# An attention and top-2 expert block on one core: the expert stage in pairs of 128 slots with two experts, in place of tiles of 256 slots with one

## The reference

```python
logits = jnp.einsum('bsh,eh->bse', x, Wr)
top_v, top_i = jax.lax.top_k(jax.nn.softmax(logits, axis=-1), 2)
top_v = top_v / jnp.sum(top_v, axis=-1, keepdims=True)
for e in range(8):
    w_e = jnp.sum(jnp.where(top_i == e, top_v, 0.0), axis=-1)
    h = jax.nn.gelu(jnp.einsum('bsh,mh->bsm', x, W1[e]) + b1[e], approximate=False)
    y = jnp.einsum('bsm,hm->bsh', h, W2[e]) + b2[e]
    out = out + y * w_e[..., None]
```

## Time and profile before

| | |
|---|---|
| median of 3 runs | 680.27 us (679.78 to 681.35) |
| the profiled execution | 680.41 us |
| its span on the core | 678.7 us |
| PE busy | 615.8 us, 91% of the span |
| DVE busy | 465.7 us, 69% |
| ACT busy | 449.9 us, 66% |
| POOL busy | 418.0 us, 62% |
| expert stage on PE | from 256.4 to 507.5 us |

### The profile page before, as it was taken

One profiled execution on the slowest core, in us unless ns is written; L12 is line 12 of the kernel. 1 busy time (PEld: TensorE's weight loads), 2 busy tenths in 40 slices (PEclk: granted clock), 3 DMA queues, 4 the chain that ended last, 5 costly groups with the idle time before them and its releaser, 6 DMA issues. The chain is left out here.

```text
span 678.7 us, 21454 instructions
## 1 busy us (share of the span) xinstructions
PE 615.8 (91%) x7417; PEld 411.7 (61%) x7417; DVE 465.7 (69%) x1312; ACT 449.9 (66%) x689; POOL 418.0 (62%) x584
## 2 busy tenths in 40 slices
PE   2877558999999999999999999999999999999965
PEld 2755323444444438999999999999984444444423
DVE  7799986766676776445545446777566687878826
ACT  3999546888888884444444444444449888888854
POOL 6355627778777787775600027677737777677771
PEclk9899968999999999999999999999999999999989
DMA  5997685655445578855432335444536375556621
GB/s 160 297 288 228 185 248 111 109 108 104 115 115 118 125 126 199 206 143 143 108 88 71 73 88 120 112 115 118 120 78 104 84 137 116 121 124 139 122 68 32
DMA packets 186592, 89.36 MB, mean 132 GB/s; under 512 B 115456, under 2 KB 176032, under 8 KB 186400
## 3 DMA queue, kind: packets, MB, share of 16 engines
q1 hardware_dynamic: 178192, 70.70, 44.7%
q0 software_dynamic: 8336, 17.84, 9.8%
HBM read 30.17 MB, written 32.24 MB: 92 GB/s over the span
## 5 line engine op out<-in xcount | busy, mean ns | idle before, releaser
L812 ACT ACTIVATE prob<-psum 128x1536 f32<-128x1536 f32 x192 | 267.2, 1453 | 64.0 <-PE psum L922 62.2
L822 ACT ACTIVATE prob<-psum,prob 128x256 f32<-128x256 f32 x284 | 117.5, 471 | 132.2 <-PE psum L1062 129.3
L648 POOL DMA_INDIRECT rows<-slot_y,idx x128 | 130.4, 1019 | 46.1 <-issue 27.2
L650 POOL DMA_INDIRECT slot_x<-rows,slots x128 | 128.2, 1001 | 36.1 <-issue 30.4
L954 PE MATMUL psum<-prob,v 128*18 128x448 f32 (+3 forms) x2048 | 137.9, 388 | 8.6 <-POOL prob L664 8.6
L664 POOL TENSOR_SCALAR_AFFINE_SELECT prob<-prob 128x384 f32<-128x384 f32 (+2 forms) x224 | 104.8, 477 | 62.6 <-ACT prob L812 60.5
L1074 PEld LDWEIGHTS psum<-prob 128*128 128x128 f32 x1136 | 137.8, 192 | 3.6
L1074 PE MATMUL psum<-prob 128*128 128x128 f32 x1136 | 138.1, 275 | 0.0
L1062 PE MATMUL psum<-xs,prob 128*128 128x256 f32 x568 | 134.8, 380 | 0.6 <-DVE xs L1468 0.4
L1062 PEld LDWEIGHTS psum<-xs,prob 128*128 128x128 f32 x568 | 102.5, 190 | 12.4 <-DVE xs L1468 0.6
L954 PEld LDWEIGHTS psum<-prob,v 128*18 128x18 f32 x2048 | 48.8, 98 | 97.0 <-issue 75.9
(11 more groups left out here) (159 smaller groups left out, 661.3 us busy)
## 6 DMA issues: line engine op xcount, KB each, us to landing
slot_y<-xs SPq DMA_DIRECT2D x71, 128.0 KB
xs<-in_L_attn_x SPq DMA_DIRECT2D x16, 256.0 KB, 4.1
prob<-in_L_ffn_W SPq DMA_DIRECT2D x16, 256.0 KB, 3.6
xn_rows<-prob SPq DMA_DIRECT2D x16, 256.0 KB, 2.7
xn_cols<-xts SPq DMA_DIRECT2D x16, 256.0 KB, 3.0
xt<-xn_cols SPq DMA_DIRECT2D x16, 256.0 KB
rows<-xn_rows SPq DMA_DIRECT2D x16, 256.0 KB, 3.5
out<-acc SPq DMA_DIRECT2D x15, 256.0 KB
```

The source lines that it names most:

```text
L648: pool.indirect_dma_start(rows[:, j, c, t, :], None, done, where).then_inc(moved[j], 16)
L650: pool.indirect_dma_start(slot_x, where, halves_of_rows[:, j, 0, t, :], None).then_inc(moved[j], 16)
L812: act.activation(prob[:, KEPT[k], :], score[k % 2], ACT.Exp, scale=SCALE / UP ** 2)\
L822: act.activation(hs[:, s, c, :], psum[:, 2 * s + c // 2, (c % 2) * FT:(c % 2 + 1) * FT], ACT.Gelu, bias=ws[:, s, B1C + c:B1C + c + 1]).the ...
```

## The change

A tile becomes a **pair** of two halves (u = 0 and 1) of 128 slots each, and each half has an expert and a set of weights of its own. An expert's slots are padded to 128, not to 256. FT is now 128 and TW, the width of a pair, 256. The number of steps falls from 71 to 68, since 16384 slots plus 8 x 127 of padding make 135 halves. The buffer `ws` of a pair holds two sets of weights, and `pick_tiles` works out 136 expert numbers in place of 71. DVE now does two `value_load`, two copies of first weights and two of second weights for a pair; `copy_x` and `copy_y` keep their size. PE's `hidden` has eight matmuls of 128x128 in place of four of 128x256, and ACT's gelus are eight of 128x128. DVE's loop has steps 4 to 41, then 26 steps are written out, again with 16 pieces of `combine` and 7 of `scale_of`. The first copy into the second weight buffer now also waits for the last attention work on the memory that it lies in. Cut to the core:

```diff
-    FT = FJ * P
+    FT, TW = P, FJ * P
-    FFN_TILES = (TOPK * NB * N + E * (FT - 1)) // FT
+    FFN_TILES = ((TOPK * NB * N + E * (FT - 1)) // FT + FJ - 1) // FJ
...
             def gelus(k, s):
-                for c in range(MC):
-                    if c % 2 == 0:
-                        act.wait_ge(hid_done, 2 * k + c // 2 + 1)
...
-                    act.activation(hs[:, s, c, :], psum[:, 2 * s + c // 2, (c % 2) * FT:(c % 2 + 1) * FT],
-                                   ACT.Gelu, bias=ws[:, s, B1C + c:B1C + c + 1]).then_inc(gelu_done, 1)
+                for u in range(FJ):
+                    act.wait_ge(hid_done, FJ * k + u + 1)
...
+                    for c in range(MC):
+                        act.activation(hs[:, s, c, u * P:(u + 1) * P], psum[:, 2 * s + u, c * P:(c + 1) * P],
+                                       ACT.Gelu, bias=ws[s][:, u, B1C + c:B1C + c + 1]).then_inc(gelu_done, 1)
...
                 def hidden(k, s):
                     pe.wait_ge(xgt_ready, k + 1)
-                    pe.wait_ge(w1_ready, k + 1)
...
-                    for c in range(MC):
-                        mm = pe.matmul(psum[:, 2 * s + c // 2, (c % 2) * FT:(c % 2 + 1) * FT],
-                                       ws[:, s, c * P:(c + 1) * P], xgt[:, s, :], start=True, stop=True)
+                    for u in range(FJ):
+                        pe.wait_ge(w1_ready, FJ * k + u + 1)
+                        for c in range(MC):
+                            mm = pe.matmul(psum[:, 2 * s + u, c * P:(c + 1) * P], ws[s][:, u, c * P:(c + 1) * P],
+                                           xgt[:, s, u * P:(u + 1) * P], start=True, stop=True)
+                        mm.then_inc(hid_done, 1)
...
             def pick_tiles():
-                stepped(dve.tensor_scalar(past[:], ends[:].rearrange("p c e -> p (c e)"), tile_at[:], None, ALU.is_le))
+                stepped(dve.tensor_tensor(past[:], of_sets(ends[:].rearrange("p c e -> p (c e)"), 3 * E),
+                                          of_parts(tile_at[:], 3 * E), ALU.is_le))
...
                 def copy_w1(k, s):
-                    e = dve.value_load(tile_i[0:1, at(k)], min_val=0, max_val=E - 1)
+                    experts = [dve.value_load(tile_i[0:1, at(FJ * k + u)], min_val=0, max_val=E - 1) for u in range(FJ)]
                     if some(k - 1):
-                        dve.wait_ge(hid_done, 2 * (k - 1))
-                        dve.wait_ge(gelu_done, MC * (k - 1))
-                    dve.tensor_copy(ws[:, s:s + 1, 0:W2C], wexp[:, at(e), 0:W2C]).then_inc(w1_ready, 1)
+                        dve.wait_ge(hid_done, FJ * (k - 1))
+                        dve.wait_ge(gelu_done, FJ * MC * (k - 1))
+                    elif known(k, 1):
+                        dve.wait_ge(weighed, CN * HALF)
+                    for u in range(FJ):
+                        dve.tensor_copy(ws[s][:, u:u + 1, 0:W2C], wexp[:, at(experts[u]), 0:W2C]).then_inc(w1_ready, 1)
...
                 def copy_w2(k, s, experts):
...
-                    dve.tensor_copy(ws[:, s:s + 1, W2C:WX], wexp[:, at(e), W2C:WX]).then_inc(w2_ready, 1)
+                    for u in range(FJ):
+                        dve.tensor_copy(ws[s][:, u:u + 1, W2C:WX], wexp[:, at(experts[u]), W2C:WX]).then_inc(w2_ready, 1)
```

More of the change, by code:

```diff
@@ L226, in build @@
         flat_xs = xs[:].rearrange("p a s t d -> p (a s t d)")
-        xg = flat_xs[:, 0:2 * FT].bitcast(U16).rearrange("p (s x n) -> p s x n", s=2, x=2)
-        xgt = flat_xs[:, 2 * FT:4 * FT].rearrange("p (s n) -> p s n", s=2)
+        xg = flat_xs[:, 0:2 * TW].bitcast(U16).rearrange("p (s x n) -> p s x n", s=2, x=2)
+        xgt = flat_xs[:, 2 * TW:4 * TW].rearrange("p (s n) -> p s n", s=2)
         xgt_halves = xgt.bitcast(U16).rearrange("p s (n x) -> p s x n", x=2)
[L230 to L234, removed]
+        ys = flat_xs[:, 4 * TW:6 * TW].rearrange("p (s j d) -> p s j d", s=2, j=FJ)
+        HS0 = FJ * WX
+        WS1 = HS0 + 2 * MC * TW
+        hs = flat_prob[:, HS0:WS1].rearrange("p (s c n) -> p s c n", s=2, c=MC)
+        ws = [flat_prob[:, w:w + FJ * WX].rearrange("p (u w) -> p u w", u=FJ) for w in (0, WS1)]
+        assert WS1 <= 3 * UW and WS1 + FJ * WX <= 5 * UW and D == P and NB * TB * E == 512
+        assert P < FJ * FFN_TILES <= 2 * P
         psum = ctx.enter_context(nc.psum_tensor("psum", [P, 8, 512], F32))
@@ L240, in build @@
         ps_last = [ps_out, psum[:, 5, :]]
-        ps_pick = psum[:, 7, 0:FFN_TILES]
+        ps_pick = psum[:, 7, 0:FJ * FFN_TILES]
         made = sem("made")
@@ L513, in between @@
                     step(k, k % 2)
-                with sp.Fori((EARLY - 1) // 2, FFN_TILES // 2 - 1) as i:
+                with sp.Fori((EARLY - 1) // 2, (FFN_TILES - 3) // 2) as i:
                     step(2 * i, 0)
                     step(2 * i + 1, 1)
-                for k in range(2 * (FFN_TILES // 2 - 1), FFN_TILES):
+                for k in range(2 * ((FFN_TILES - 3) // 2), FFN_TILES):
                     step(k, k % 2)
@@ L705, in at_tile @@
                 elif phase == 3:
-                    count = counted_by(pool, MC * (k + 1))
+                    count = counted_by(pool, FJ * MC * (k + 1))
                     pool.wait_ge(made, 1)
@@ L1037, in body @@
                         pe.wait_ge(proj_evac, TB * (b + 2))
-                        pe.matmul(ps_pick, pick[:], identh[:, 0:FFN_TILES], start=True, stop=True).then_inc(picked, 1)
+                        for j in range(FJ):
+                            rest = min(P, FJ * FFN_TILES - P * j)
+                            mm = pe.matmul(ps_pick[:, P * j:P * j + rest], pick[:, j], identh[:, 0:rest], start=True, stop=True)
+                        mm.then_inc(picked, 1)
                     elif k == 9:
@@ L1335, in pick_tiles, with of_sets, of_parts @@
             def pick_tiles():
[L1336 to L1337 removed]
+                def of_sets(ap, n):
+                    return ap.rearrange("p (a n) -> p a n", a=1).broadcast_to([P, FJ, n])
+                def of_parts(ap, n):
+                    return ap.rearrange("p (j a) -> p j a", a=1).broadcast_to([P, FJ, n])
+                stepped(dve.tensor_tensor(past[:], of_sets(ends[:].rearrange("p c e -> p (c e)"), 3 * E),
+                                          of_parts(tile_at[:], 3 * E), ALU.is_le))
+                stepped(dve.tensor_tensor(past[:], past[:], of_sets(weight[:], 3 * E), ALU.mult))
                 stepped(dve.tensor_reduce(expert[:], past[:], AX.X, ALU.add))
[L1339 removed]
+                dve.tensor_tensor(pick[:], of_sets(ones[:], P), of_parts(expert[:], P), ALU.mult).then_inc(pick_ready, 1)
             def write_plan():
```

53 lines of the change are left out of this document (25 added, 28 removed).

## The result

The changed kernel takes **715.79 us** in the median of 4 runs (714.57 to 717.49), the kernel before 680.02 us (678.23 to 681.35, 4 runs): a ratio of 1.0529, 95% interval 1.0509 to 1.0549. It is slower, as forecast, but by 35.8 us and not by 21; the time lies 2.8 us above the range.

What follows compares the result with a forecast made beforehand. PE bounded the expert stage before; after the change, DVE's work between `outputs` and a later `hidden` would. Terms -7.3 + 17.9 + 8.4 + 3 = +22, taken as +21 on 680.41, gave 701.5 us, range 688 to 713.

Steps and rivals of the forecast that it cites:

- The chain named: DVE's ordered work from the end of `outputs(k-1)` to `hidden(k+2)`, in the expert stage; if longer than PE's step, PE stalls.
- two steps take (step + C): Expert stage: when C exceeds PE's step, two steps last PE's step plus C, so the mean step is half that.
- C: Time from the end of `outputs(k-1)` to the earliest `hidden(k+2)` DVE allows; 3.23 us before, forecast 4.50 after the loop's branch.
- the first four steps: Start of the expert stage: later first `hidden`, waits for the last attention batch and behind `share_gates`; together +3 us.
- Hidden additions: Rival: DVE's added loads and copies are hidden and PE keeps the pace; 674 us, chance 0.06.
- cheap loads: Rival: the second load runs wholly beside the copies, C 3.70 in the loop; 683 us; loads costing less had chance 0.10.
- a lower clock: Rival: PE, idle for an eighth of the stage, gets a lower clock and a 6% longer step; 709 us, chance 0.05.
- The far upper end: Rival: 1.10 us a load and 0.41 each second-weight copy, C 5.08 in the loop; 715 us, chance 0.07.
- The 26 written-out steps: Steps behind DVE's loop: 16 with `combine`, 7 with `scale_of`, 3 bare, all over PE's 3.56 us; +8.4 us.
- With `combine`: 16 written-out steps: both second copies count in full, C 3.99, or 4.1 with late loads; mean step 3.83 us.
- With `scale_of`: 7 written-out steps: both second copies and the second load count, C 4.67; mean step 4.12 us.
- The loop's term: 38 steps of DVE's loop: C 4.50, mean step 4.03, 0.47 us over PE's; +17.9 us.

Runs made afterwards that it cites:

- e2_one_load: The changed kernel with one `value_load` a pair, both halves getting the first half's expert weights; 694.66 us, ratio 1.0197 to the kernel before.
- e8_three_loads: The changed kernel with a third `value_load` per pair whose value nothing uses; 742.91 us, ratio 1.0916 to the kernel before.
- e3_one_copy: The changed kernel with both loads but only the first half's first and second weights copied; 695.58 us, ratio 1.0219 to the kernel before.
- e4_unroll: The changed kernel with only DVE's loop written out, loads, copies and their order kept; 702.69 us, ratio 1.0324 to the kernel before.
- e5_hoist: The changed kernel with DVE's loop written out and pair k+2's loads issued between `copy_x(k+1)` and `copy_y(k-1)`; 683.48 us, ratio 1.0041 to the kernel before.
- e9_ahead: e5_hoist with `combine` halves and `scale_of` in their old steps but issued ahead of `copy_y`; 679.61 us, ratio 0.9989 to the kernel before.
- e6_moved: e5_hoist with `scale_of` moved to the former loop steps and `combine` in 3, 3 and 2 rows ahead of `copy_y`; 673.82 us, ratio 0.9916 to the kernel before.
- e1_split: The kernel before with `hidden` as eight 128x128 matmuls, DVE and ACT unchanged; 690.48 us, ratio 1.0146 to the kernel before.

## Why the prediction was right in the loop and short behind it

**Right.** The chain named is the one that binds. In the loop *two steps take (step + C)* shows in the alternation, and C was forecast at 4.50 and is 4.46 in the turn shown. Each part of C was tested by itself: loads (e2_one_load, e8_three_loads), copies (e3_one_copy), the loop's arithmetic and branch together (e4_unroll). Moved off the chain, the loads cost nothing in the steps that were the loop (e5_hoist). The prices of a load, 0.8 us in the loop and 0.6 written out, were near: from one TENSOR_LOAD of a pair to the next it is 0.72 and 0.63 us (medians of 38 and 25 pairs in the trace after). PE's step is 3.57, forecast 3.56, and the first four steps put pair 4 at 271.81 against 269.37, +2.4 where +3 stood.

By the Trainium skill (Perfetto Trace Analysis, Sequencer-only Instruction) a profile has only the execution of such an instruction, not its fetch and decoding nor its waits. The trace agrees in that durations alone fall short: they make 310 + 190 + 23 = 523 ns, while 0.63 us pass from load to load in written-out code. What fills the rest, no run here shows.

**The rivals.** Hidden additions (674) and cheap loads (683) fall with C. So does a lower clock as the cause of the longer stage: it was granted at 1.00 from 275 us to the end of the stage. Half of that, 1.2 GHz, was granted only from 271.7 to 275.1, behind the waits of the first steps; that stretch lies in one step, of 5.24 us (271.81 to 277.06). The far upper end, 715, has the right time by the wrong reason: it needed C = 5.08. By the Trainium skill (SBUF — State Buffer, the "DVE blocks DMA" trap) copies on DVE in a two-port mode hold up DMAs that POOL issues; the prediction worked that out to 705. In the trace POOL's fetches inside the stage take 1032 ns in the median after and 1002 before, and 946 and 945 behind it. So they are somewhat longer beside DVE's copies, but the additions that need the fetched rows hardly wait. The group of `combine`, shapes kept apart, in the whole changed kernel:

```profile
L1408 DVE SCALAR_TENSOR_TENSOR acc<-rows,gate,acc 128x128 f32<-128x128 f32 x96 | 29.8, 373 | 0.3
```

DVE is idle for 0.3 us ahead of these 96 additions. That does not exclude the rule, but it is not where the time went.

**Wrong: the size, 9.4 us up to the end of the stage.** The term "*The 26 written-out steps*, +8.4" is the step that failed. The mean of 25 of them is 4.15 us, not 3.88, which makes 6.5 us. Two things in it were wrong.

With `combine` the term took C at 3.99 to 4.1, because "the engine works without a gap" there. In the trace after, these steps come mostly as 3.67 and 4.57 in turn, and C is the longer of the two. In it DVE has a gap of 0.34 us, where the prediction allowed 0.2; the second load of that pair took 484 ns (306 in the earlier trace rows). The two first-weight copies take 0.78 us up to `copy_x`, 0.44 more than one did, where 0.34 was forecast. The mean of 14 such steps is 4.11 us, not 3.83.

With `scale_of` C was forecast long enough, 4.67 against 4.27 to 4.60. What failed is the halving, *two steps take (step + C)*. That rule needs DVE to be at `copy_y` when PE ends `outputs`. Here DVE comes late, `copy_y` waits for nothing, and DVE's own row of loads, copies and additions sets every step: 4.47 us from one second-weight copy to the next (454.03 to 458.50), beside PE's 4.48. The mean of the 7 steps is 4.41 us, not 4.12. e9_ahead shows the same limit with the loads out of the way: 3.72 us for a step with `combine`, over PE's 3.57.

The loop's term, +17.9, was short by 4.0 us: the mean of its 38 steps is 4.14, not 4.03. A step behind a stall takes PE 3.67 us and not 3.56: a `hidden` that had to wait takes 2.05 us, one that had not takes 1.95. `copy_x` releases PE after 0.22 us (350.75 + 0.45 to 351.42), not 0.14. And the first turns, and some up to 348 us, have a C of up to 4.8 us; the longest second loads, 0.56 to 0.61 us (last section), fall in such turns. The start was some 0.6 us better than forecast. With it and the rounding of the parts the end of the stage is out by 9.4.

**Wrong by what the prediction did not look at: 3.7 us behind the stage**, 174.1 against 170.5 in the two profiled executions. The window shown has a granted clock of 0.89 in the last 78 us, 0.94. In the trace after, the clock falls to half twice ahead of the last microseconds (657.4 to 664.3 and 688.1 to 695.0 us), in the trace before once (655.3 to 662.1). The stretch that is new, columns as in the earlier trace rows:

```profile
657.40:664.30 6.90, 6.90 (x74) 2.14 (x76) 1.35 (x5) 4.79 (x4) 3.21 (x6) 0.51 0.09 23
```

PE is busy through it, so at half the clock it loses some 3.4 us (an estimate from this row). The waits of the stage are not needed for it: e6_moved, whose PE hardly waits in the stage, has 0.89 and 174.2 us there, e5_hoist 0.93 and 170.5. The clock is not the whole of what sets that length either, since e1_split has 174.0 us at 0.93. What brings the second stretch was not tried.

701.5 + 9.4 + 3.7 gives 714.6, and the profiled execution took 714.57.

## What to carry to other kernels

A half-idle engine can still set the pace: look for the work that it does, in order, between a result that it waits for and the buffer that it hands on, and compare that with the other engine's step, its sequencer's register loads and address arithmetic included, which no busy share counts. Here each `value_load` in such a chain costs 0.6 to 0.7 us per two steps, and a loop's address arithmetic and branch together as much. Writing the loop out and issuing the loads a step early, where the engine waits anyway, brought back 32 us of 36. The price of a chain may be halved over two steps only as long as the engine is back in time for the other's next result. Where its own row of work is longer than the other's step, that row is the step: here the order gave half of what was left behind the loop, and spreading the work the other half.

## What the runs showed of the hardware that was not expected

**Stretched loads.** A TENSOR_LOAD takes 298 to 606 ns for one number in the changed kernel. In e2_one_load the long ones all lie early in the stage. Source line L1459 while POOL sends rows, and later, while POOL fetches rows:

```profile
L1459 DVEq TENSOR_LOAD <-tile_i x17: 304/318/630, 282.7 to 344.9; - x17
```

```profile
L1459 DVEq TENSOR_LOAD <-tile_i x29: 303/308/320, 402.2 to 510.0; - x29
```

POOL issues indirect DMAs in both stretches, and two loads of 588 and 589 ns follow its last sending (342 us). In after, loads of up to 508 ns come between 350 and 413 us, while it issues none. So these DMAs do not explain them. The cause stays open; no run separated it.

**The loop's arithmetic and branch**, for addresses that are known when the code is written out, cost 0.6 us for two steps, as much as a load.

**Runs differ behind the stage** by more than the stage's own edits suggest: in the eleven traces it is 169.9 to 176.3 us from the stage's end to the last instruction. e1_split's excess, and the width of e9_ahead's runs (675.34 to 682.46), are of this size. The twelve runs of e9_ahead go with the clock granted over the run: 675.3 to 678.9 us at 0.974 or more, 681.0 to 682.5 at 0.969 or less. A theory of a stage is better tested on the stage's own length than on the total.
